# Closing one long fused kernel differently: who adds the last states, who sends the LayerNorm scales, who weighs the one-hot groups

## What is computed

```
x = x + linear_attention(layernorm(x))
x = x + ffn(layernorm(x))        # router one
x = x + state_space(layernorm(x))
x = x + ffn(layernorm(x))        # router two

ffn:  logits = tokens @ Wr + br               # 8 experts
      expert = argmax(softmax(logits)); p = max prob
      y = relu(tokens @ W1[expert] + b1) @ W2[expert] + b2;  out = y * p
state_space:  state = exp(dt*A) * state + dt*B*u + 1e-6     # 512 channels x 16 states, over time
      y = sum_n(state_n * C_n) + D*u;  y = y * silu(z);  out = y @ out_w.T
```

## Time and profile before

| | us |
|---|---|
| median of 3 runs (lowest, highest) | 1498.74 (1496.77, 1501.54) |
| span of the profiled execution, first to last instruction | 1497.7 |
| PE busy | 1367.7 (91%) |
| DVE busy | 1032.2 (69%) |
| ACT busy | 953.2 (64%) |
| POOL busy | 850.7 (57%) |
| mean granted TensorE clock | 0.950 of full |

### The profile page before, as it was taken

One profiled execution on the slowest core, in us unless ns is written; L12 is line 12 of the kernel. 1 busy time (PEld: TensorE's weight loads), 2 busy tenths in 40 slices (PEclk: granted clock), 3 DMA queues, 4 the chain that ended last, 5 costly groups with the idle time before them and its releaser, 6 DMA issues.

```text
span 1497.7 us, 22073 instructions
## 1 busy us (share of the span) xinstructions
PE 1367.7 (91%) x6962; PEld 959.9 (64%) x6962; DVE 1032.2 (69%) x1557; ACT 953.2 (64%) x1765; POOL 850.7 (57%) x413
## 2 busy tenths in 40 slices
PE   5999998999998988989989989999899878769997
PEld 3566686999644555555655655556556676559996
DVE  6666533333334899899889989998998998843332
ACT  1222221444326999998998998999989989104442
POOL 1111002555101897887888878878878878325552
PEclk9999988999999999999999999999999879959999
DMA  9200035766500797997997998979969989467662
GB/s 301 78 28 28 29 86 162 206 207 211 173 12 17 161 226 159 203 221 155 211 221 156 215 197 179 219 171 204 214 147 210 219 196 214 113 194 218 210 209 82
DMA packets 108374, 249.45 MB, mean 167 GB/s; under 512 B 19113, under 2 KB 49966, under 8 KB 94064
## 3 DMA queue, kind: packets, MB, share of 16 engines
q0 software_dynamic: 23248, 133.01, 40.9%
q1 hardware_dynamic: 74688, 113.61, 25.5%
q10 hardware_dynamic: 10336, 1.54, 0.6%
HBM read 116.72 MB, written 18.94 MB: 91 GB/s over the span
## 4 chain that ended last, share of the span: by engine, by line
PE 60%; DVE 12%; ACT 11%; issue 9%; DMA 4%; POOL 2%; ACTq 1%; another core or an unknown queue 0%; DVEq 0%; POOLq 0%
PE ps L1518 11%; PE ps L1263 9%; PE ps L1458 9%; PE ps L1467 9%; DVE arena L1161 4%; ACT arena L706 4%; ACT arena L716 4%; PE ps L1549 4%; PE ps L1288 4%; PE ps L1325 2%; PE ps L1383 2%; PE ps L1279 2%; PE ps L1593 2%; PE ps L1413 2%; POOL arena L469 2%
## 5 line engine op out<-in xcount | busy, mean ns | idle before, releaser
L469 POOL TENSOR_TENSOR arena<-arena 128x2048 f32<-128x2048 f32 x97 | 446.9, 4607 | 152.1 <-DVE arena L1161 143.2
L1161 DVE TENSOR_TENSOR_SCAN arena<-arena,ps 128x512 f32<-128x512 f32 x392 | 471.6, 1213 | 62.0 <-PE ps L1263 48.9
L1263 PEld LDWEIGHTS ps<-cst,arena 128*128 128x128 f32 x2428 | 308.3, 148 | 308.2 <-issue 199.0
L1263 PE MATMUL ps<-cst,arena 128*128 128x128 f32 x2428 | 379.7, 285 | 70.3 <-ACT arena L716 33.6
L706 ACT ACTIVATE arena<-arena,a_neg 128x512 f32<-128x512 f32 x512 | 367.4, 718 | 49.1 <-DVE arena L1161 37.7
L716 ACT ACTIVATE arena<-arena,m_bt 128x512 f32<-128x512 f32 x512 | 364.1, 712 | 2.8 <-DVE arena L1092 1.7
L1518 PE MATMUL ps<-arena,tapw 128*128 128x512 f32 x512 | 260.5, 609 | 0.0
L1037 DVE TENSOR_TENSOR arena<-ps,arena 128x256 f32<-128x256 f32 x78 | 33.2, 425 | 205.3 <-PE ps L1467 121.7
L437 POOL DMA_INDIRECT arena<-rows,arena x78 | 75.9, 973 | 167.0 <-DVE arena L1017 143.8
L1161 DVE TENSOR_TENSOR_SCAN x<-arena,ps 128x512 f32<-128x512 f32 x120 | 143.9, 1211 | 19.3 <-PE ps L1263 14.3
L1458 PEld LDWEIGHTS ps<-arena 128*128 128x128 f32 x1248 | 153.0, 194 | 4.5 <-ACT arena L614 0.5
(11 more groups left out here) (160 smaller groups left out, 1569.7 us busy)
## 6 DMA issues: line engine op xcount, KB each, us to landing
arena<-arena POOLq DMA_DIRECT2D x52, 1024.0 KB, 8.4
arena<-in_W SPq DMA_DIRECT2D x94, 512.0 KB, 8.2
x<-arena POOLq DMA_DIRECT2D x33, 1024.0 KB, 8.5
arena<-c_rows SPq DMA_DIRECT2D x128, 256.0 KB, 3.7
arena<-x POOLq DMA_DIRECT2D x16, 1024.0 KB, 9.1
rows<-x SPq DMA_DIRECT2D x16, 512.0 KB, 4.4
x<-x POOLq DMA_DIRECT2D x8, 1024.0 KB, 8.7
x<-residual SPq DMA_DIRECT2D x12, 512.0 KB, 5.8
```

What stands on the lines that cost most here:

```text
L469: g.tensor_tensor(h, h, m_c[i % RC].unsqueeze(1).to_broadcast([P, KI, SEQ]), ALU.mult)\
L1161: v.tensor_tensor_scan(out=h[:, k, :], data0=m_a[g % RA], data1=ps[SCAN_BANK[g % 3]][:, :], initial=0.0, op0=ALU.mult, op1=ALU.add).then_i ...
L1263: return t.transpose(bank, src[:, k * P:(k + 1) * P], ident)
```

## The change

Five edits: (1) product 124 isn't added by a transfer any more (`add_on` ends one state earlier), and TensorE adds it with four more `y_sum` matmuls; the order of TensorE's work is new, and `logits(1, 6)` moves behind the last `y_sum`. (2) SP sends the last C row two states earlier. (3) `scales_out` moves from ACT's queue to SP's; in round 0 behind the eight row stores and ahead of `ipw` and `conv`, in round 1 behind the loads of the expert weights. (4) POOL does the product L1006 for three of the four groups (`weigh_hot`), between its waits for `f_h` and its gathers; DVE keeps the fourth. (5) `f_hot` counts POOL's three, `f_end` the fourth.

```diff
@@ SP
+            def scales_out(r):
+                half = RING * SEQ
+                sp.wait_ge(S("f_scales"), r + 1)
+                for i in range(2):
+                    lo = half * (i ^ r)
+                    sp.dma_start(xs[r][lo:lo + half, D:ROW].rearrange("(c p) v -> p c v", p=P),
+                                 scales[:, i * NCH // 2:(i + 1) * NCH // 2, :]).then_inc(S("scales_out"), 16)
...
             for b in range(BATCH):
                 sp.wait_ge(S("a_xupd"), b + 1)
                 store_rows(0, b)
+            scales_out(0)
             sp.wait_ge(S("row_zeroed"), 32)
             sp.dma_start(ipw, T["ip_x"].rearrange("(k p) d -> p k d", p=P)).then_inc(S("ld_cw0"), 16)
...
-                    if b == BATCH - 1 and n == NS - 2:
+                    if b == BATCH - 1 and n == NS - 4:
                         sp.wait_ge(S("f_tr"), BATCH + IN_LAST)
                         sp.dma_start(c_end, c_rows[b % 2][NS - 1].partition_broadcast(P)).then_inc(S("m_c_end"), 16)
+                    if b == BATCH - 1 and n == NS - 2:
                         break
...
             load_ffn(sp, 1)
+            scales_out(1)
             send_w1(1)
@@ POOL
+            def weigh_hot(r):
+                for i in range(NCH // GROUP - 1):
+                    g.wait_ge(S("f_h"), NCH // GROUP * r + i + 1)
+                    if i >= 2:
+                        g.wait_ge(S("f_inv"), NCH // GROUP * r + i - 1)
+                    g.tensor_tensor(r_val[i % 2], r_h[i % 2].unsqueeze(2).to_broadcast([P, GROUP, NV, COLS]),
+                                    vals[:, GROUP * i:GROUP * (i + 1), :].unsqueeze(3).to_broadcast([P, GROUP, NV, COLS]),
+                                    ALU.mult).then_inc(S("f_hot"), 1)
...
+            weigh_hot(0)
             send_tiles(0)
...
                 c_product(i)
-                if i % NS >= 2 and i < BATCH * NS - 3:
+                if i % NS >= 2 and i < BATCH * NS - 4:
                     add_on(i)
...
+            weigh_hot(1)
             send_tiles(1)
@@ ACT
-            def scales_out(r):
-                half = RING * SEQ
-                a.wait_ge(S("f_scales"), r + 1)
...
-                if i == BATCH - 2:
-                    scales_out(0)
...
             def feed(r):
-                if r:
-                    scales_out(r)
                 a.wait_ge(S("f_lg"), 2 * r + 1)
@@ DVE
-                    link(v.tensor_tensor(r_h[i % 2], iota.unsqueeze(1).to_broadcast([P, GROUP, COLS]),
-                                         r_hi[:, cs].unsqueeze(2).to_broadcast([P, GROUP, COLS]), ALU.is_equal))
-                    v.tensor_tensor(r_val[i % 2], r_h[i % 2].unsqueeze(2).to_broadcast([P, GROUP, NV, COLS]),
-                                    vals[:, cs, :].unsqueeze(3).to_broadcast([P, GROUP, NV, COLS]), ALU.mult)\
-                        .then_inc(S("f_hot"), 1)
+                    v.tensor_tensor(r_h[i % 2], iota.unsqueeze(1).to_broadcast([P, GROUP, COLS]),
+                                    r_hi[:, cs].unsqueeze(2).to_broadcast([P, GROUP, COLS]), ALU.is_equal)\
+                        .then_inc(S("f_h"), 1)
+                    if i == NCH // GROUP - 1:
+                        v.wait_ge(S("f_h"), NCH // GROUP * (r + 1))
+                        v.tensor_tensor(r_val[i % 2], r_h[i % 2].unsqueeze(2).to_broadcast([P, GROUP, NV, COLS]),
+                                        vals[:, cs, :].unsqueeze(3).to_broadcast([P, GROUP, NV, COLS]), ALU.mult)\
+                            .then_inc(S("f_end"), 1)
@@ PE
-                    t.wait_ge(S("f_hot"), NCH // GROUP * r + i + 1)
+                    if i < NCH // GROUP - 1:
+                        t.wait_ge(S("f_hot"), (NCH // GROUP - 1) * r + i + 1)
+                    else:
+                        t.wait_ge(S("f_end"), r + 1)
...
             t.wait_ge(S("m_xupd"), 2 * (BATCH - 1))
+            for half in (range(2), range(2, KI)):
+                t.wait_ge(S("m_cp"), end - 3)
+                if half[0]:
+                    t.wait_ge(S("m_sz"), KI * BATCH)
+                for k in half:
+                    y_sum(H[end - 4], k, True, False)
+                t.wait_ge(S("m_chain0"), chained(end - 6))
+                for k in half:
+                    y_sum(H[first], k, False, False)
             t.wait_ge(S("m_chain1"), chained(end - 5))
             for k in range(KI):
-                if k == 2:
-                    t.wait_ge(S("m_sz"), KI * BATCH)
-                y_sum(H[first + 1], k, True, False)
+                y_sum(H[first + 1], k, False, False)
             x_turn(1, BATCH - 2)
-            t.wait_ge(S("m_chain0"), chained(end - 4))
-            for k in range(KI):
-                y_sum(H[first], k, False, False)
-            logits(1, BATCH - 2)
             t.wait_ge(S("m_cp"), end - 1)
             for k in range(KI):
                 y_sum(H[end - 2], k, False, True)
+            logits(1, BATCH - 2)
             t.wait_ge(S("f_raw"), 2 * BATCH - 1)
```

More of the change, by code:

```diff
@@ L565, in raw_copy @@
                     .then_inc(S("f_raw"), 1)
-            def scales_out(r):
-                half = RING * SEQ
-                a.wait_ge(S("f_scales"), r + 1)
-                for i in range(2):
-                    lo = half * (i ^ r)
-                    a.dma_start(xs[r][lo:lo + half, D:ROW].rearrange("(c p) v -> p c v", p=P),
-                                scales[:, i * NCH // 2:(i + 1) * NCH // 2, :]).then_inc(S("scales_out"), 16)
             for i in range(2):
```

## The result

The changed kernel took 1505.57 us in the median of 20 runs (1497.26 to 1508.13), the kernel before 1499.47 beside it on the same chip; the ratio of the two is **1.0029, 95% interval 1.0016 to 1.0043**, that is +2.4 to +6.4 us. The forecast was +4.2 us. On another chip, unaltered, the changed kernel came to 1.0037 [1.0016, 1.0058]. It is slower, by about as much as can be told at all. One of the kernel before's twenty runs, at 1641.81 us, was slow and counts in its median but not in the ratio.

A forecast was written before the change was run, and what follows sets the result against it. PE's queue was taken to bound the recurrence's end and router two's groups, DVE router one's. Terms 0.8 + 3.2 + 0.2 = +4.2 us on 1498.74 gave 1502.9 us, range 1496.5 to 1509.

The forecast's parts named there:

- The products on POOL: Both routers' groups: POOL and DVE block each other both ways, 1.53 us per product; router one +3.2, router two +0.2 including scales.
- the reading by one direction alone: Both routers: only DVE is blocked and POOL starts at once; about +1.2 and -0.7 instead of +3.2 and +0.2.
- The scales on SP: Router two: the exponential no longer stands behind ACT's issuing of the scales, DVE's next limit is PE's count; -1.64 us.
- Router one: SP issues the scales ahead of `conv`, which still lands before PE's tap; taken as 0, upper bound +2.7 us.
- The end of the recurrence: Last state input to out matmuls: stalls of 2.87 us go, four new matmuls cost 3.54; +0.8 us, bounds +0.3 and +1.2.
- cover gone: nothing: End of the recurrence: with the earlier C row, DVE's products and pair sums end 1.5 us before they are needed.
- A: POOL pays more for short rows, 3 us per product instead of 1.5; +11.8 us, 1510.5; chance 0.15.
- B: POOL and DVE don't block each other at these shapes; +1.0 us, 1499.7; chance 0.17.
- C: PE is granted 2.4 GHz in both routers' groups; some -3 us, 1495.7; chance 0.08.
- D: `conv` is late in router one; +2.7 us on top, 1505.6; chance 0.06.
- E: End of the recurrence: DVE's removed 3.97 us wait was the bound; -4 instead of +0.8, 1498.1; chance 0.04.

The follow-up runs named there:

- experiment 4: Changed kernel with the comparisons' lane and column tables copied to PSUM, so each comparison has one SBUF input; ratio to the kernel before 1.0005 [0.9978, 1.0032].
- the tail alone: Kernel before with only the end-of-recurrence edits (four more sums on TensorE, new order, last C row two states earlier); ratios 1.0038 and, repeated, 1.0022.
- experiment 3: Changed kernel with the one-hot products back on DVE, keeping the end-of-recurrence edits and the scales on SP; ratio to the kernel before 1.0000 [0.9978, 1.0022].

## Why the prediction was right, point by point

**The total.** 1502.9 was forecast, +4.2 us (+0.28%), leaning to slower; measured were +0.29% and +0.37%. That they agree so well is luck in part. The forecast is a sum of stages, and against it stand +1.94 for router one's groups and 1.15 for `conv` (+3.2 and 0 forecast), +0.25 for the tail in the first profile and up to +2.8 in others (+0.8), and -0.33 for router two, scales included (+0.2). The stages of the two profiles shown add up to 1.7 to 2.85 us, not to 4.2. What the time holds beyond that isn't explained.

**The products on POOL: mechanism right, size too large.** The forecast reasoned from one operation of 0.16 us that had been held for 2.18 to a block in both directions: first `r_lo` against POOL, then POOL against `r_h`. Both are in the trace, at each place named, and experiment 4 shows the cause by taking one SBUF input away. The Trainium skill (SBUF — State Buffer, "SBUF: two separate sides") states this as exclusive for the whole instruction, whoever starts first; by that rule, the traces agree: 2.17 = 0.9 of waiting + 1.26, 1.55 = 1.07 + 0.48. It is these durations that decide between one direction and two, not the totals: the reading by one direction alone gave +1.2 and -0.7, the forecast +3.2 and +0.2, and with +1.94 and -0.33 measured the one-direction totals lie nearer, for a wrong reason. Two sizes made the forecast too large. The product's price was 1.53 from a line through the earlier trace rows, and 1.26 was measured; rows of 40 elements cost no extra. That made router two +1.39 for the products instead of +1.84, and it goes into the 0.9 us by which router one's last group was ready sooner behind its first `r_lo` (11.35 us instead of 12.2). The other size is the clock: the forecast had group 2 slow as well, 0.85 us that didn't come, and the last group at 3.28 where it took 3.71. Together that is +1.9 instead of +3.2. But +3.2 is also what router one shows where the clock would otherwise have stayed up. The forecast took that fall for given in both kernels; the nine profiles without the products say that it comes within the groups in three of them.

**The scales on SP: right.** -1.64 forecast, -1.72 measured, and up to -2.5 against other executions of before, since ACT's issuing varies. DVE's next limit was PE's count, as read from the earlier trace rows. **Router one:** 0 with an upper bound of +2.7 for a late `conv`; it was 1.15 where the logits ended early, 0 in the four other profiles with this order on SP. The step that put it at 0 took 5.7 us more for the issue and 7.9 for the landing. `conv` was issued 5.25 us later (203.93), but PE had to wait until 10.6 us behind that, longer than the 10.2 of the upper bound.

**The end of the recurrence: the step that failed is "+0.8 (bounds +0.3, +1.2)".** Four sums took 3.43 us from start to start, not 3.54. Against the profile shown it is +0.25, just under the lower bound: the out matmuls stand at 1296.09, and the forecast had 1296.1, but the whole stretch had come 0.58 later. Against other executions it is anything from nothing to 2.76. The two waits of 1.00 and 1.44 were read as a fixed stall of 2.44 us that the change would swap for 3.54 us of matmuls. It was slack, and in an execution where PE is late it is zero (13.82 us with the old tail, 16.58 with the new one), while the four added matmuls cost 3.4 us always. The bounds came from one execution's durations, not from what its waits would be in another. Nor was "cover gone: nothing" right for the early C row: DVE's closing products met POOL's last one, and in one profile of eight they came too late for PE.

**The rivals.** A (3 us per product): out, 1.26. B (no block): out. C (the clock turns to 2.4 GHz in both routers' groups): out. Router two's groups ran at a granted 0.50 as before, and router one's last group at 1.2 GHz. D: in part. E (the removed wait bounded): out. DVE waits 3.28 us for PE in its place.

**What stays open.** The times of kernels with more matmuls at the end are higher than their stages say: +0.22 and +0.38% for the tail alone where the profiles give 1.9 us (0.13%) at most in the mean, and +0.58% where they give 3.3 at the most. It may be chance in six to twelve runs, or a stage that these profiles didn't catch; the experiments don't tell.

## What to carry to other kernels

A wait in one profile is not a sum of time to be traded: ask what sets it, and whether an engine that arrives later would find it gone. Work put in its place costs in every execution, while the wait is there only in some. Before handing a two-input product from DVE to POOL, list what DVE does at the same moment; if those operations read two SBUF tiles, the engines take turns and both lose (here 0.82 us of DVE's became 2.17 of POOL's and 1.55 for a 0.48), unless one of DVE's inputs lies in PSUM. And a part that gains 1.7 us in every profile, like the scales here, needs more than five rounds to be seen in the time.

## What the runs showed of the hardware that was not expected

**TensorE's clock falls at another moment in another execution, while TensorE is busy without a break.** Router one's logits are matmuls of 8 columns, back to back. In the first profile of before the granted clock fell to 1.2 GHz between 203 and 205 us (0.79 there, 1.00 ahead of it, 0.50 behind it), with PE busy all the time from 199 on. In experiment 3 PE was at 1.2 GHz from 191 already, back at 2.4 for a few us, and fell again at about 203. The rows, before and then experiment 3:

```profile
200.93 1.85 PE L1383 MATMUL ps<-wr,arena 128*128 128x8 f32 x16
208.00 6.83 PE L1383 MATMUL ps<-wr,arena 128*128 128x8 f32 x32
```

```profile
191.37 6.07 PE L1324 MATMUL ps<-arena 128*128 128x256 f32 x16
206.48 3.42 PE L1382 MATMUL ps<-wr,arena 128*128 128x8 f32 x16
216.51 6.83 PE L1382 MATMUL ps<-wr,arena 128*128 128x8 f32 x32
```

Sixteen instructions take 1.85 us at 2.4 GHz and 3.42 at 1.2. The last logits were ready for DVE at 213.7 to 215.5 us in four of the profiles and at 221.0 to 223.7 in the other ten, whatever had been edited. That is a swing of 5.5 to 10 us in one stage, more than the whole effect studied here. It needn't reach the end, though. In the kernel before they were ready at 215.2 in one profile and at 221.4 in the other; the first scans of the recurrence started at 472.4 and 475.6, the last but one update of x at 1238.2 and 1238.1, and both spans are 1497.7 us. The times of one kernel range over 9 to 16 us on one chip (before: 1491.5 to 1505.1 on one chip, 1495.8 to 1510.1 on another), and what makes that range isn't shown.

**The out matmuls right behind the sums fell to 1.2 GHz in two of eight profiles with the tail's edits** (8.83 us for the 32 instructions, above, and 8.86 in experiment 4, instead of 7.17 to 7.34), for a part of their time, and in none of the six with the old one. With the old tail it fell among the sums in two of six (5.40 and 6.73 us, above), where PE had waited 1.97 and 1.61 us for a transfer just before.
